# Which engine makes the low half of a group's inputs in the shared part of an expert stage

## The reference, cut to what matters

```python
sg = xf @ shared_gate_w.T
su = xf @ shared_up_w.T
shared_out = jax.nn.silu(sg) * su @ shared_down_w.T
topk_idx, w, _scores = _route(xf, router_w, correction_bias)
...
return (shared_out + routed).reshape(B, T, C)
```

## Time and profile before

| what | value |
|---|---|
| median of 3 runs | 3039.66 us (3037.16 to 3042.45) |
| the profiled execution: its time, its span | 3042.53 us, 3040.8 us |
| part one of the expert stage | 1660 to 1966 us |
| busy in that stretch of 306 us: PE, DVE, POOL, ACT | 276.96, 242.18, 202.09, 131.26 us |
| mean granted TensorE clock, whole span | 0.942 of full |

### The profile page before, as it was taken

One profiled execution on the slowest core, in us unless ns is written; L12 is line 12 of the kernel. 1 busy time (PEld: TensorE's weight loads), 2 busy tenths in 40 slices (PEclk: granted clock), 3 DMA queues, 4 the chain that ended last, 5 costly groups with the idle time before them and its releaser, 6 DMA issues. The chain is left out here.

```text
span 3040.8 us, 62014 instructions
## 1 busy us (share of the span) xinstructions
PE 2701.5 (89%) x20141; PEld 2315.6 (76%) x20141; DVE 2168.6 (71%) x4904; ACT 1818.7 (60%) x4791; POOL 2010.0 (66%) x2179
## 2 busy tenths in 40 slices
PE   6999999999999999999997899899998932288897
PEld 5888888888888888888886788688887811166775
DVE  5767676777676677777664888544455668889997
ACT  5666666666666666666664444233335744199996
POOL 4888888788888888888885676622223400178886
PEclk9999999999999999999997999999999965599999
DMA  8665656565566666665555110112223560011111
GB/s 221 114 112 109 113 114 114 104 114 115 113 113 115 109 112 118 113 109 112 108 110 119 38 37 30 48 50 58 58 55 114 170 111 0 16 28 49 44 35 42
DMA packets 684347, 270.86 MB, mean 89 GB/s; under 512 B 602809, under 2 KB 657057, under 8 KB 684034
## 3 DMA queue, kind: packets, MB, share of 16 engines
q1 hardware_dynamic: 677362, 248.34, 40.3%
q0 software_dynamic: 6672, 18.55, 1.6%
HBM read 100.16 MB, written 32.39 MB: 44 GB/s over the span
## 5 line engine op out<-in xcount | busy, mean ns | idle before, releaser
L844 POOL COPY attention_probT<-attention_planesT 128x1024 uint16<-128x1024 uint16 x512 | 676.5, 1367 | 181.3 <-PE attention_turns L422 109.3
L529 ACT ACTIVATE attention_prob<-attention_turns,attention_neg_max 128x256 f32<-128x256 f32 x1024 | 467.6, 481 | 228.3 <-DVE attention_neg_max L682 227.6
L835 POOL COPY attention_planes<-attention_prob 128x1024 uint16<-128x1024 uint16 x512 | 527.2, 1060 | 20.8 <-ACT attention_prob L529 20.8
L682 DVE TENSOR_REDUCE attention_neg_max<-attention_turns 128x2 f32<-128x512 f32 x512 | 317.9, 683 | 184.6 <-PE attention_turns L407 184.5
L383 PE MATMUL attention_turns<-kv_hi,wkv 128*128 128x512 f32 x1024 | 374.9, 407 | 0.0
L351 PE MATMUL attention_turns<-wkv,kv_hi 128*128 128x512 f32 x1024 | 315.5, 389 | 1.9 <-ACT attention_prob L529 1.9
L422 PE MATMUL attention_turns<-attention_probT,attention_v 128*64 128x128 f32 x4096 | 257.7, 280 | 2.4 <-issue 2.4
L518 ACT COPY attention_v<-attention_turns 128x512 f32<-128x512 f32 x256 | 150.5, 590 | 182.5 <-PE attention_turns L351 182.4
L698 DVE TENSOR_TENSOR attention_turns<-attention_turns,attention_attT_lo 128x512 f32<-128x512 f32 x128 | 139.8, 1092 | 147.6 <-DMA attention_attT_lo<-inverse_rows 142.2
L422 PEld LDWEIGHTS attention_turns<-attention_probT,attention_v 128*64 128x64 f32 x4096 | 226.5, 139 | 20.1 <-issue 3.7
L383 PEld LDWEIGHTS attention_turns<-kv_hi,wkv 128*128 128x128 f32 x1024 | 193.4, 189 | 55.4 <-issue 21.6
(11 more groups left out here) (407 smaller groups left out, 8122.3 us busy)
## 6 DMA issues: line engine op xcount, KB each, us to landing
attention_attT_lo<-inverse_rows SPq DMA_DIRECT2D x256, 128.0 KB, 3.0
experts_rows<-rows_in SPq DMA_DIRECT2D x69, 132.5 KB, 2.3
attention_ctx<-in_ctx SPq DMA_DIRECT2D x32, 256.0 KB, 3.2
attention_planesT<-attention_planes SPq DMA_TRANSPOSE x512, 3.2
far_ctxT<-in_ctxT SPq DMA_DIRECT2D x16, 512.0 KB, 4.2
far_routed_rows<-rows_out SPq DMA_DIRECT2D x16, 512.0 KB, 4.6
weights_ctx<-in_ctx SPq DMA_DIRECT2D x16, 512.0 KB, 3.8
out<-conv_x_out SPq DMA_DIRECT2D x15, 512.0 KB, 2.8
```

The source lines that it names most:

```text
L529: made = act.activation(prob[n % 2][:, h, :], bank_of("s", 2 * n + e)[:, m * 256:(m + 1) * 256], ACT.Exp, bias=neg_max[:, n % 2, 2 * e + m ...
L682: made = dve.tensor_reduce(neg_max[:, n % 2, 2 * e:2 * e + 2], bank_of("s", 2 * n + e)[:, :].rearrange("p (h c) -> p h c", h=2), AX.X, ALU ...
L835: pool.tensor_copy(planes[n % 2][:, g, :, :], words.rearrange("p (c b) -> p b c", b=2)).then_inc(planes_made, 1)
L844: pool.tensor_copy(words.rearrange("p (c b) -> p b c", b=2), planesT[:, g, :, :]).then_inc(joined, 1)
```

## The change

`low_x`, one subtraction of 128x1024 float32 numbers, goes from POOL's program to DVE's. On POOL it stood behind `low_hidden` and ahead of `scatter`. On DVE it stands behind the unit's multiply and `add_out`, and ahead of the routing. What it waits for (`xT_high`, from ACT's `high_x` of the same unit) and what it signals stay the same.

```diff
+            def low_x(e):
+                s = place_in_order(e) % 2
+                dve.wait_ge(xT_high, highs_before(e) + 1)
+                tt(xT_lo[s][:, :, :], xT[:, :, :], xT_hi[s][:, :, :].bitcast(F32), ALU.subtract
+                   ).then_inc(xT_split, 1)
...
                 if n >= 2 and (n - 2) % STILES == STILES - 1:
                     add_out((n - 2) // STILES)
+                if high_due(n):
+                    low_x(high_due(n))
                 if due("groups", n):
                     route_groups(due("groups", n))
...
-            def low_x(e):
-                s = place_in_order(e) % 2
-                pool.wait_ge(xT_high, highs_before(e) + 1)
-                pool.tensor_tensor(xT_lo[s][:, :, :], xT[:, :, :], xT_hi[s][:, :, :].bitcast(F32), ALU.subtract
-                                   ).then_inc(xT_split, 1)
...
                 low_hidden(n)
-                if high_due(n):
-                    low_x(high_due(n))
                 if due("measure", n):
```

## The result

The change took 3045.19 us (median of 19 runs, 3039.38 to 3051.33) against 3039.66 us for the kernel before, measured on the same chip (median of 19 runs). The medians differ by 5.5 us. The ratio of the two kernels over all these runs is 1.0023, 95% interval 1.0016 to 1.0031. The profiled execution took 3043.46 us, its span 3041.7 us.

A forecast was written before the change was run, and what follows sets the result against it. DVE, stalled by POOL's low half, was taken to set the triples' time. Triples 9.5, first triples and unit 43 0.5, tail -2.0 gave +8 us on 3039.66: 3048 us, range 3045 to 3053 (8 in 10: 3041 to 3055).

The forecast's parts named there:

- The step that decides: DVE's low half waits 2.8 us for ACT's high half, inside the loop, with picks and next multiply queued behind.
- B: Three part-one triples with a low half (units 12, 24, 36): forecast +1.4 us each.
- C: Three part-one triples with a low half (units 15, 27, 39): forecast +1.6 us; one already slow charged 0.3.
- The replay: Step-by-step retiming of the three kinds of triple from measured durations; allowed to be off 0.3 us in each of nine.
- T: PE's turn in a triple; forecast low half at T+3.4, picks at T+4.6, next multiply about T+7.5.
- A: Three part-one triples with a low half (units 9, 21, 33): forecast +0.6 us each.
- "same" rival: POOL's hidden low halves miss the classes in nine triples, saving 0.9 to 1.2 us each: within 0.2%, chance 0.30.
- The clock: Worse branch: PE's pause grows in six triples; if four drop in clock, total +10 to +12 us.
- the triples that I had put at zero: Part-one triples from units 6, 18 and 30, which make no low half: forecast no change.
- The end of part one: From unit 48's low half to the last pad scatter, POOL is the path: -2.0 us, between -2.4 and 0.
- the smaller gain of 1.4 us: In part one's tail, if DVE's low half held POOL's scatter up, -2.0 us would become about -1.4.
- The total: Whole kernel: +8 us, to 3048 us; more than 0.2% slower had chance 0.64.

The follow-up runs named there:

- e1: The change with DVE's low half moved behind the ten steps of picks: 3038.53 us, ratio to the kernel before 0.9982.
- e2: The kernel before, low half on POOL, plus only DVE's wait for ACT's high half where the change has it: 3059.02 us, ratio to before 1.0054.
- second trace: The change and the kernel before, each run once more unchanged for another trace: 3044.31 and 3030.57 us.
- e3: The kernel before with only unit 48's low half moved to DVE, the other twelve on POOL: 3038.32 us, ratio to before 0.9985.
- e6: The kernel before, low half on POOL, with only add_out moved to its unit's end in units without a groups step: 3049.26 us, ratio 1.003.
- e10: The change with low half behind the picks and add_out at its unit's end in units without a groups step: 3032.03 us, ratio to before 0.9972.
- e4: The change with DVE's low half put one unit later, behind that unit's multiply and add_out: 3042.49 us, ratio to before 1.0002.

## Why the prediction was right, and which terms were off

**The step that decides held.** The high half is ready 3.2 us behind the turn, DVE waits 2.75 us for it in B and C, and ten steps of picks stand behind. e1 moves only the place and C falls by 2.1 us; e2 keeps only the wait (with POOL's stall behind it), and the loss is 16.4 us against 17 expected. The loss of 0.8 to 1.4 us in the B and C triples, and PE's pause of 2.6 to 3.0 us at full clock, are close to what I forecast. One C is the exception in the first traces, with nothing: before had a lowered clock in it, which alone was worth 1.25 us.

**The replay was late by 0.2 us.** I put the low half at T+3.4 and the next multiply at T+7.5. In the triple turned at 1807.20 they came at T+3.20 and T+7.32. ACT's high half began at T+2.11, not T+2.23. So B is +1.0 to +1.3 rather than +1.4, and C +0.8 to +1.4 rather than +1.6.

**A was charged three times too much:** +0.2 against +0.6. In A and C one class instruction was stalled as expected (in the trace of the change, this one in the A from unit 21):

```profile
1798.63 1.21 DVE L1470 TENSOR_TENSOR experts_picked<-experts_picked,experts_group_neg 128x32 f32<-128x32 f32 x1
```

A row of 1.21 to 1.22 us stands in all six A and C triples, in both traces. I had expected one of over 1 us in all nine, and in B that failed. In the first trace its L1456 took 0.96 us twice and 0.45 once. In the second trace no class instruction of a B was held at all: there `add_out` waited 0.6 to 0.9 us for PE, and the classes began when POOL's hidden low half was over. In the B from unit 24 they started at T+10.08, where before they started at T+8.27: nothing of the later multiply was absorbed, and nothing was stalled. These 1.8 us are near the 1.9 of my sum (1.6 less 0.6, and 0.9 of stall), but come about another way, and B cost 1.2 us there against 1.0 to 1.3 in the first trace.

The "same" rival needed the stalls to miss the classes and time to be won by it. In A and C they hit, and where they missed, in B, nothing was won. (By its own terms that rival comes to -1.6 us, not to "about -1": 8 less 3.6, 2.7 and 3.3.) The total alone wouldn't exclude it, since the interval of the ratio reaches down to 0.16%.

**The clock was put in the wrong place.** I charged a lowered clock to the six triples with the long pause. It did fall more often (between the turns of units 9 and 42: four stretches of 3.4 us in the first trace of the change and two in the second, against one and none of before), but what it cost fell on the triples that I had put at zero. The windows at 1772.77, 1844.65 and 1845.27 make no low half, have no idle time on PE, and took 17.08, 16.98 and 16.96 us at a mean clock of 0.90, where PE's floor is 15.5. That is +1.5 us each: three in two traces. e3, which has no long pause, has one such triple too (17.15 us), and e6 has one of 17.14 us. Three more stretches of lowered clock in e6 fell on A triples whose pauses, 1.6 to 1.7 us, are those of before. So it isn't shown that the lowered clocks come from the change. The C at 1825.62, with a pause of 2 us left in it, paid only 0.4 over its kin at full clock. These +1.5 to +3.0 us made good what A, B and C fell short of. The sum was right partly by luck.

**The end of part one** gave -2.7 and -2.5 us from the turn of unit 48, against -2.0 with a bound of -2.4. The stretch ahead of this turn is 0.5 to 0.6 us longer with the change, and POOL's work doesn't move with it: counted from the turn of unit 42, the last pad ends 2.0 us earlier, as the replay had it, in both traces of the change and in e3. Here are the scatter of unit 48, DVE's low half beside it, and the last pad, for comparison with the earlier trace rows:

```profile
1950.50 1.10 POOL L1635 DMA_INDIRECT rows_in<-experts_rows,experts_places  x1 [0.29 <-POOL experts_rows L1632]
1950.64 1.22 DVE L1522 TENSOR_TENSOR second_xT_lo<-first_xT,second_xT_hi 128x1024 fp32r<-128x1024 f32 x1 [2.75 <-ACT second_xT_hi L1299]
1951.91 0.96 POOL L1635 DMA_INDIRECT rows_in<-experts_rows,experts_places  x1 [0.30 <-issue]
...
1966.31 0.96 POOL L1641 DMA_INDIRECT rows_in<-experts_zero_rows,experts_pad_places  x1 [0.30 <-issue]
1972.56 0.66 PE L1195 MATMUL experts_misc<-ident,experts_rows 128*128 128x128 f32 x2 [5.98 <-issue]
```

The first scatter began 0.14 us ahead of the low half, the second 0.05 us behind its end. Neither was lengthened, so the smaller gain of 1.4 us did not come. Where a scatter does begin under the low half, it is held (last section).

**The total.** The traces give +7.2 and +8.2 us in part one, the ratio of the runs 7.0. Outside part one, single executions of one kernel differ by as much: the two traces of before reach the first turn of part one at 1669.6 and 1661.5 us. So the difference of two profiled executions (0.9 us between the first pair, 13.7 between the second) says little, and part one had to be compared by itself.

## What to carry to other kernels

An engine's busy time is not the price of an instruction that it is given. What counts is the place in its program: a subtraction that waits for a copy, put ahead of work that is ready, cost about 1 us a triple; ten steps later, behind that work, it gained. When a wait is taken away, look for the next one in the same engine's order (here the addition, which waited for PE), and read the whole stretch to its end before counting the gain: 3 us won ahead of a turn can be lost behind it.

## What was not expected of the hardware

**A DVE instruction from SBUF holds up a scatter that begins under it.** The rows of the scatters (L1637) and the low half of e10 in two places:

```profile
1902.36 0.96 POOL L1637 DMA_INDIRECT rows_in<-experts_rows,experts_places  x1 [0.30 <-issue]
1903.63 1.79 POOL L1637 DMA_INDIRECT rows_in<-experts_rows,experts_places  x1 [0.30 <-issue]
...
1933.21 1.32 POOL L1637 DMA_INDIRECT rows_in<-experts_rows,experts_places  x1 [0.30 <-issue]
```

```profile
1903.37 1.23 DVE L1522 TENSOR_TENSOR first_xT_lo<-first_xT,first_xT_hi 128x1024 fp32r<-128x1024 f32 x1 [2.04 <-ACT first_xT_hi L1299]
...
1932.47 1.23 DVE L1522 TENSOR_TENSOR second_xT_lo<-first_xT,second_xT_hi 128x1024 fp32r<-128x1024 f32 x1 [3.29 <-ACT second_xT_hi L1299]
```

The low halves end at 1904.60 and 1933.70. The scatters begun under them end at 1905.42 and 1934.53, both 0.82 to 0.83 us behind that end, and are longer by 0.83 and 0.36 us than their usual 0.96. It is no accident of two rows: over all traces 52 scatters begin within 1.05 us of the start of a DVE low half and under it, and every one ends 0.83 to 0.84 us behind its end. A scatter that began just ahead of the low half kept its length (1.10 us at 1950.50 above). In the nine triples of the change's first trace only one scatter was lengthened by more than 0.02 us: 1.27 us at 1830.09. The Trainium skill, SBUF — State Buffer, section "SBUF: two separate sides", says that a DVE instruction holding the shared ports keeps GpSimd from writing its descriptors, and names it for two-port performance modes. Of a `tensor_tensor` with both inputs in SBUF, which the low half is, the same section says only that it contends with GpSimd's reads, and that a probe did not see it stall a DMA. These rows differ from that, by up to 0.83 us a time, and the prediction applied the rule to the low half without this restriction. Whether the scatter is held at its read of the places from SBUF or at its descriptors, no run here tells.

**The two engines hold each other up both ways.** DVE's low half takes 1.22 us alone and 2.14 us when POOL's 1.30 us subtraction is running as it begins (e4 above). From the start of the one (1816.84) to the end of the other (1819.23) is 2.39 us, near the 2.52 us that they take one after the other. The same stands once in the change, where the low half of unit 43 took 2.07 us. The other way it is less: a POOL subtraction that begins under DVE's low half takes 1.54 to 1.55 us in place of 1.30, three times in e4. One of them:

```profile
1675.25 1.22 DVE L1522 TENSOR_TENSOR second_xT_lo<-first_xT,second_xT_hi 128x1024 fp32r<-128x1024 f32 x1
1676.08 1.55 POOL L1625 TENSOR_TENSOR experts_hidden_lo<-experts_weighed,experts_hidden_hi 128x512 fp32r<-128x512 f32 x1 [4.23 <-ACT experts_hidden_hi L1319]
```
